# Weighing the values on quarter tiles in two PSUM banks, later in the slot, and without the loop over layers

## The reference

```python
def local_attention(q, k, v):              # 16 heads of 64, window w = 32
    ...                                    # bq: windows of 32 queries
    bk2, bv2 = (look(bk), look(bv))        # a window and the one before it: 64 keys
    sim = jnp.einsum('bhwie,bhwje->bhwij', bq, bk2) * QK_SCALE
    sim = jnp.where(mask, -jnp.finfo(sim.dtype).max, sim)
    attn = jax.nn.softmax(sim, -1)
    out = jnp.einsum('bhwij,bhwje->bhwie', attn, bv2)
    return out.reshape(b, h, n, d)
...
for i in range(DEPTH):                     # 6
    x = attn_layer(shift_tokens(x), Wqkv[i], q_scale[i], k_scale[i], Wo[i]) + x
    x = ffn_layer(shift_tokens(x), ln_g[i], ln_b[i], W1[i], b1[i], W2[i], b2[i]) + x
```

## Time and profile before

| what | value |
|---|---|
| median of 3 runs | 2080.57 us (2078.74 to 2081.38) |
| the profiled execution | 2075.03 us |
| its span, first to last instruction | 2073.2 us |
| PE busy | 1919.3 us (93%) |
| DVE busy | 1605.8 us (77%) |
| ACT busy | 1390.0 us (67%) |
| POOL busy | 1341.2 us (65%) |

### The profile page before, as it was taken

The page is one execution under the profiler, slowest core; times in us unless marked ns, Lnnn a source line. Parts: engine busy times, 40 slices in busy tenths (PEclk is TensorE's granted clock), DMA queues, the critical chain, the costliest instruction groups (busy, mean ns, idle before and its releaser), DMA issues. The chain is left out here.

```text
span 2073.2 us, 70057 instructions
## 1 busy us (share of the span) xinstructions
PE 1919.3 (93%) x26905; PEld 1408.2 (68%) x26905; DVE 1605.8 (77%) x3109; ACT 1390.0 (67%) x2780; POOL 1341.2 (65%) x1402
## 2 busy tenths in 40 slices
PE   4999997899999999989989999998999899999995
PEld 3667665777767767767767677676777676777762
DVE  5666665788898878888868988688888788888773
ACT  2665663677757767776767577676777675777762
POOL 0000004998788767878767977688878678787840
PEclk9999999999999999999999999999999999999996
DMA  2000000443424334333343243343333433333330
GB/s 95 2 1 0 0 30 6 115 107 101 123 76 105 96 92 119 90 90 96 98 112 100 75 104 98 90 121 88 91 100 96 116 93 79 103 99 96 98 91 20
DMA packets 190633, 171.70 MB, mean 83 GB/s; under 512 B 32160, under 2 KB 186440, under 8 KB 190152
## 3 DMA queue, kind: packets, MB, share of 16 engines
q1 hardware_dynamic: 190280, 167.02, 30.7%
HBM read 21.14 MB, written 1.05 MB: 11 GB/s over the span
## 5 line engine op out<-in xcount | busy, mean ns | idle before, releaser
L407 POOL TENSOR_TENSOR z_raw<-rot_u,rot_v 128x256 f32<-128x256 f32 x768 | 552.2, 743 | 186.3 <-DVE rot_v L1016 183.8
L422 POOL TENSOR_TENSOR z_norm<-probs_t,z_raw 128x512 f32<-128x512 f32 x384 | 493.1, 1306 | 110.4 <-DVE probs_t L1065 110.4
L1015 DVE TENSOR_TENSOR rot_u<-bank,tabs 128x512 f32<-128x512 f32 x384 | 263.1, 685 | 183.3 <-ACT sq L521 180.2
L781 PE MATMUL bank<-x_high,w_high 128*128 128x256 f32 x768 | 304.4, 396 | 2.8 <-issue 1.1
L553 ACT ACTIVATE pair_bank<-pair_bank 128x512 f32<-128x512 f32 x192 | 111.8, 582 | 256.1 <-DVE pair_bank L998 255.9
L521 ACT ACTIVATE sq<-bank 128x512 f32<-128x512 f32 x384 | 225.6, 589 | 53.9 <-PE bank L783 44.4
L1016 DVE TENSOR_TENSOR rot_v<-bank,tabs 128x512 f32<-128x512 f32 x384 | 261.5, 681 | 0.0
L428 POOL TENSOR_TENSOR sqs<-sq 128x512 f32<-128x512 f32 x192 | 245.3, 1278 | 23.6 <-POOL z_norm L422 23.5
L540 ACT ACTIVATE probs_t<-bank 64x512 f32<-64x512 f32 x384 | 227.3, 592 | 45.4 <-PE bank L760 43.1
L772 PEld LDWEIGHTS bank<-probs_t,v_late 128*64 128x64 f32 x3072 | 155.5, 138 | 145.8 <-issue 145.8
L825 PE MATMUL bank<-sqs,consts 128*128 128x512 f32 x384 | 204.4, 614 | 44.5 <-POOL sqs L428 41.5
(11 more groups left out here) (153 smaller groups left out, 4545.4 us busy)
## 6 DMA issues: line engine op xcount, KB each, us to landing
zqk<-z_norm SPq DMA_DIRECT2D x1536, 64.0 KB, 2.1
v_late<-v_sb SPq DMA_DIRECT2D x192, 192.0 KB, 2.6
w_qkv<-in_L_ffn_Wqkv SPq DMA_DIRECT2D x18, 512.0 KB, 5.1
v_late<-v_sb SPq DMA_DIRECT2D x192, 32.0 KB, 2.2
wo<-in_L_ffn_Wo SPq DMA_DIRECT2D x24, 128.0 KB, 2.1
w<-in_L_ffn_W SPq DMA_DIRECT2D x12, 170.5 KB, 3.0
consts<-in_constants SPq DMA_DIRECT2D x1, 1088.0 KB, 5.1
w_qkv<-in_L_attn_w_kv_up SPq DMA_DIRECT2D x2, 512.0 KB, 6.3
```

The costliest lines, as they stand in the source:

```text
L407: a = pool.tensor_tensor(z_raw[:, parity, idx, half, :], rot_u[:, idx, half, :], rot_v[:, idx, 1 - half, :], ALU.add)
L422: a = pool.tensor_tensor(z_norm[:, parity, idx, :, :], rinv[:, idx, :].unsqueeze(1).broadcast_to([P, 2, T]), z_raw[:, parity, idx, :, :], ...
L781: pe.matmul(dst, w_high[:, j, cols], x_high[:, odd, :], start=True, stop=False)
L1015: dve.tensor_tensor(rot_u[:, idx, :, :], src, tabs[:, 2 * idx, :, :], ALU.mult)
```

## The change

Two edits are made. First, the probabilities are copied as they are, not spread among zeros, by one copy of 128 partitions; V is then weighed by 32 products in place of 16, each of 64 keys by 64 features with 32 moving columns, on four tiles of 64 by 64. The products of the lower keys' half go to `B_T`, those of the upper half to `B_K`, so ACT copies the outputs in two pieces of 256 columns. Because `B_K` is used, the products must wait until the keys in it were squared, and `weigh_windows` moves behind the MLP and the queries; on ACT the squares of the keys move ahead of the logarithm. Second, `stream` runs all slots as straight code; register arithmetic becomes constants, the `sem_inc` of `room_met` and `split_begun` and the memset of `spread` go.

```diff
-        def stream(eng, slot):
-            for k in range(FIRST, LOOP):
-                slot(k, 0)
-            with eng.Fori(0, TURNS) as r:
-                for k in range(LOOP, LOOP + LAYER):
-                    slot(k, r)
-            for k in range(LOOP, LAST - TURNS * LAYER):
-                slot(k, TURNS)
...
+        def stream(slot):
+
+            for s in range(FIRST, LAST):
+                slot(s)
...
                     act.wait_ge(S["turned"], s)
                     after(act, "lpv_done", s - 1)
-                    tiles = B_T.rearrange("p (h s c) -> p h s c", h=HG, s=TILES)
-                    for x in range(2):
-                        rows = slice(KEYS * x, KEYS * x + KEYS)
-                        a = act.activation(spread[rows, :, :, WIN * x:WIN * x + WIN], tiles[rows, :, :, :], ACT.Copy)
-                    a.then_inc(S["spread_ready"], 1)
...
+                    a = act.activation(turned_t[:, :, :], B_T.rearrange("p (h c) -> p h c", h=HG), ACT.Copy)
+                    a.then_inc(S["turned_ready"], 1)
...
+                if one:
+                    squares(s + 4, "k_prod", B_K, 1, "k_square")
                 if two:
                     m = s + 3
                     act.wait_ge(S["n_done"], m + 1)
...
-                if one:
-                    squares(s + 4, "k_prod", B_K, 1, "k_square")
...
-                    act.activation(yt[:, 2 * og:2 * og + 2, :], B_T.rearrange("p (c t) -> p c t", c=2), ACT.Copy).then_inc(S["lyt_ready"], 1)
+                    for x, bankx in enumerate((B_K, B_T)):
+                        dst = yt[:, 2 * og:2 * og + 2, :].rearrange("p c (t x n) -> p c t x n", t=TT, x=2)
+                        a = act.activation(dst[:, :, :, 1 - x, :], bankx[:, 0:T].rearrange("p (c t n) -> p c t n", c=2, t=TT), ACT.Copy)
+                    a.then_inc(S["lyt_ready"], 1)
...
-                pe.wait_ge(S["spread_ready"], n + 1)
-                for pair, tile, a in itertools.product(range(2), range(TILES), range(2)):
-                    h, t = 2 * pair + a, tile // 2
+                pe.wait_ge(S["turned_ready"], n + 1)
+                for pair, tile, a, x in itertools.product(range(2), range(TILES), range(2), range(2)):
+                    h, t, rows = 2 * pair + a, tile // 2, slice(KEYS * x, KEYS * x + KEYS)
                     f = slice(g * GW + h * D, g * GW + (h + 1) * D)
-                    y = B_T[D * a:D * a + D, T * pair:T * pair + T].rearrange("p (t x s c) -> p t s x c", t=TT, x=2, s=2)
-                    mm = pe.matmul(y[:, t, tile % 2, :, :], (v_sb if tile % 2 else v_late)[:, odd, t, f], spread[:, h, tile, :], start=True, stop=True,
-                                   tile_position=(0, D * a), skip_group_check=True)
+                    at = P * pair + WIN * tile
+                    mm = pe.matmul((B_T, B_K)[x][D * a:D * a + D, at:at + WIN], (v_sb if tile % 2 else v_late)[rows, odd, t, f],
+                                   turned_t[rows, h, WIN * tile:WIN * tile + WIN], start=True, stop=True, tile_position=(KEYS * x, D * a), skip_group_check=True)
...
-                if four:
-                    weigh_windows(s - 1, unit_of(k - 1, r), (k - 1) % G, (k - 1) // G % 2)
...
                 if one:
                     project(s + 4, 0, B_Q, g, odd, "lq_done", ("q_prod", "q_square"))
+                if four:
+                    if one:
+                        pe.wait_ge(S["k_square"], s + 5)
+                    weigh_windows(s - 1, (s - 1) // G, (s - 1) % G, (s - 1) // G % 2)
                 if one:
                     values(s + 4, g, odd)
```

More of the change, by code:

```diff
@@ L367, in slot @@
-                if k == LAYER + 14:
-                    sp.wait_ge(S["mlp_done"], (NB // 2) * (r + 1))
-                    sp.sem_inc(S["room_met"], 1)
-                    down_weights(r + 1)
-            stream(sp, slot)
+                    out_weights(0, s + 1)
+                l = layer_begun(s, LAYER - 14)
+                if l:
+                    sp.wait_ge(S["split_done"], G * l)
+                    qkv_weights(l)
+                for g in range(G):
+                    l = layer_begun(s, LAYER - 1 + g)
+                    if l:
+                        sp.wait_ge(S["lwo_done"], s - 1)
+                        out_weights(l, g)
@@ L374, in _ @@
+            stream(slot)
             sp.wait_ge(S["scores_done"], GROUPS)
@@ L428, in slot @@
                     pool.tensor_tensor(sqs[:, :, :], sq[:, :, 0, :], sq[:, :, 1, :], ALU.add).then_inc(S["sums_ready"], 1)
-                    rotated(s + 4, k % 2, 0, "q_prod", "q_summed")
-                if not isinstance(r, int) and LAYER - 7 <= k < LAYER - 7 + G:
-                    g = k + 7 - LAYER
-                    if g == 0:
-                        pool.wait_ge(S["w_in"], 16 * 3 * (r + 2))
-                    pool.wait_ge(S["lv_done"], s + 4)
-                    pool.sem_inc(S["split_begun"], 1)
-                    split_weights(r + 1, g)
-            pool.wait_ge(S["pv_done"], STEPS)
-            pool.memset(spread[:, :, :, :], 0.0).then_inc(S["spread_zero"], 1)
+                    rotated(s + 4, s % 2, 0, "q_prod", "q_summed")
+                for g in range(G):
+                    l = layer_begun(s, LAYER - 7 + g)
+                    if l:
+                        pool.wait_ge(S["w_in"], 16 * 3 * (l + 1))
+                        pool.wait_ge(S["lv_done"], s + 4)
+                        split_weights(l, g)
             pool.wait_ge(S["w_in"], 16 * 3)
@@ L442, in _ @@
                 split_weights(0, g)
-            stream(pool, slot)
+            stream(slot)
         @block.scalar
@@ L604, in _ @@
             gate_biases(0)
-            act.wait_ge(S["spread_zero"], 2)
-            stream(act, slot)
+            act.wait_ge(S["late_zero"], 1)
+            stream(slot)
         @block.tensor
@@ L899, in _ @@
                 pt_taken(STEPS - 1, h)
-            stream(pe, slot)
+            stream(slot)
             for p in range(PAIRS):
@@ L1036, in out_biases, with slot @@
                 dve.wait_ge(S["out_bias_ready"], l + 1)
-            def slot(k, r):
-                s, g = LAYER * r + k, k % G
-                one, two, three = active(k, r, -4, GROUPS - 4), active(k, r, -3, GROUPS - 3), active(k, r, 0, GROUPS)
-                if k % (2 * G) == 5 and mlp_active(k, r, 21):
-                    p, b = mlp_of(k - 21, r), 2 * ((k - 21) // (2 * G)) % NB
+            def slot(s):
+                g = s % G
+                one, two, three = active(s, -4, GROUPS - 4), active(s, -3, GROUPS - 3), active(s, 0, GROUPS)
+                if mlp_slot(s, 21):
+                    p = (s - 21) // (2 * G)
+                    b = 2 * p % NB
                     dve.wait_ge(S["mlp_done"], p + 1)
@@ L1101, in _ @@
             turn(causal, 0, ("post",))
-            stream(dve, slot)
+            stream(slot)
             dve.wait_ge(S["mlp_res"], MLPS)
```

250 lines of the change are left out of this document (120 added, 130 removed).

## The result

The changed kernel takes 2107.16 us, median of 4 runs (2104.17 to 2116.16), beside 2079.65 for the kernel before in the same session (2073.41 to 2081.38). The ratio is 1.0145, 95% interval 1.0108 to 1.0182: 1.45% slower. The profiled execution took 2106.53 us, with a span of 2104.7 against 2073.2.

A forecast was written before the change was run, and what follows sets the result against it. PE, busy 93%, was taken to bound the kernel, each slot being its work plus small waits. Loop -31, new waits +70, first slots and tables +10 gave +49: 2124 beside the profiled 2075.03, median 2130 us, range 2055 to 2170.

The forecast's parts named there:

- Loop: Where the stream jumps back: straight code saves 7.8 us at each of four jumps, -31 us; bounds 0 and -31.
- Block: The weighing's 64 pairs on four tiles: each turn bound by its 64-column load, 1.06 us, so halved matmuls buy nothing.
- The weakest step: Weighing block: the load-bound turn, resting on a slope of mean durations; named weakest together with slots 0 to 3.
- The short block: Rival, 0.14: four tiles give the scores' rate, block 0.78 us in place of 1.06, 24 us less in all, 2106.
- the long one: Rival, 0.05: loads or tiles of the two row halves take turns, block 1.9 us; 2290 at most, 2210 likelier.
- My second rival: The weighing block near its lower bound, the scores' 64 pairs in 0.78 us, by the skill's promised speedup; chance 0.14.
- Slot by slot, per eight: New PE waits after the weighing moves behind MLP and queries: +3.2 us per eight slots, +70 over 22 eights.
- The waits: PE waits for gate copy (slots 6, 7, about 0.8), keys' squares (slot 5, 0.7), output copy (starts of slots 5, 6).
- 0.8 is new: Slot 6, before the centre product: 1.54 us from the weighing's end, values hide 0.72, leaving 0.8 of new wait.
- First slots and tables: First slots, and five times where DVE writes new rotary tables and the logarithm waits for late keys: +10 us.
- The rival "faster": Chance 0.18: new waits replace 1.9 us of old ones per eight; 2089, 2064 or 2050 us; eights below 68.0 mean faster.

The follow-up runs named there:

- the two halvings: Changed kernel with loads of 32 columns in place of 64: 2084.14 us; changed kernel with 16 moving columns in place of 32: 2109.13 us; one run each.

## Why the prediction was right, and by how much it missed

The forecast was 2130 us, +2.4%; measured were 2107.16, +1.45%. The direction and both mechanisms hold; the sum over the slots was too large.

**Loop: -31.** Measured were -29.6 in the jumps' slots, and -31.5 between the medians of straight code and the kernel before. Right.

**Block: 1.06 us, bound by its loads.** Measured 1.065, and the two halvings show the reason. The weakest step was the surest. The short block and the long one fall. The Trainium skill, "TensorEngine Tiling (Array Packing)", section "Theoretical Speedup", gives up to double where a dimension is 64 or less. Counted by pairs the trace agrees: 1.082 / 32 = 33.8 ns a pair before, 16.6 after. But there are twice as many pairs, since a product no longer serves two windows at once, and so the block gained 1.6% (1.082 to 1.065 us). My second rival had read a rate of pairs as a time of the block.

**Slot by slot, per eight.** The first column is the prediction's, the second is the typical slot after less before:

| slots | forecast | measured |
|---|---|---|
| 4 | +0.23 | +0.08 |
| 5 | +0.95 | +0.80 |
| 6 | +0.67 | +0.60 |
| 7 | +0.82 | +0.75 |
| 0 and 1 | +0.3 | +0.16 |
| 2 and 3 | +0.2 | +0.13 |
| sum | +3.2 | +2.5 |

Every term has the right sign and is too large, by 0.07 to 0.15. One mis-sized step stands in slots 4, 6 and 7: I took 1.08 us out of PE's chain ahead of MLP and queries. A tiled block costs something at its edges as well. The norm's next product comes after 0.86 us when it is the MLP (1545.40 to 1546.26), and came after 0.95 when it was the block; the queries begin 0.46 after the MLP's product (1546.26 to 1546.72), before it was 0.56 (1103.69 to 1104.25):

```profile
1104.25 0.68 PE L781 MATMUL bank<-x_high,w_high 128*128 128x256 f32 x1
```

That is 1.27 us, not 1.08; back in come 0.08, as the block begins 0.20 after the last product of the queries (1556.58 to 1556.78) instead of 0.12, and 0.10 in the values behind it (1541.23 to 1541.45, where 0.12 is usual). PE's work stays the same in sum, but 1.27 - 0.08 = 1.19 left the front of the slot, so the block starts 0.1 earlier than I worked out, and with it all that waits for its end. In slot 7 I had queries done at 5.79; the block starts at 1565.58 - 1559.87 = 5.71. In slot 4 it starts at 1540.16 - 1532.73 = 7.43 where I had 7.63, of which the edges are half. In slot 6 two errors nearly cancel: I had queries done at 6.24, but the kernel before starts its values 7.50 into that slot (1106.09 to 1113.59), so that it should have been 7.50 - 1.08 = 6.42; the block starts at 1556.78 - 1550.59 = 6.19, as the wait for POOL's sums fell there from 0.36 to 0.22 besides. Slot 5 hangs on the squares of the keys and not on PE's chain (below), and slots 0 to 3 I have not followed row by row. The Trainium skill, "TensorEngine Tiling (Array Packing)", section "Key Properties", says that changing the tiling mode drains TensorE. It gives no price; the rows here put 0.08 to 0.1 us on an edge, and whether the drain is the cause they can't show.

**The waits.** The waits for the gate copy and for the squares of the keys are there; the one for the output copy doesn't show as I had said. The chain from the block's end to the centre product was forecast at 1.54 and is 1559.36 - 1557.85 = 1.51. I said "0.8 is new"; the profile prints 0.54, since it counts from the modelled end of the last product, but the distance between the products grew by 0.70, as the kernel with the gate copy first shows. The wait for the squares of the keys in slot 5 was forecast at 0.7 and is 0.60: ACT starts them 5.77 after the slot's start (forecast 5.8), and they release PE 0.65 later (forecast 0.58 and a wake of 0.16):

```profile
1547.94 0.60 ACT L505 ACTIVATE sq<-bank 128x512 f32<-128x512 f32 x1 [0.60 <-DVE rot_v L1000]
```

So the block began 6.42 into slot 5 and not 6.54, most of that slot's 0.15. The waits for the output copy I had put at the starts of slots 5 and 6; the view prints none there. From the block's end to the next transposes it is 1542.17 - 1541.23 = 0.94 us, beside 0.96 to 0.98 in the forecast, but 0.82 of it are now values, so the wait is about 0.1 where I had 0.26.

**First slots and tables: +10.** Slots 0 to 15 grew by 3.5, and 4.6 came ahead of slot 0. The layers' last slots grew by 9.1; five times slots 2 to 7 at the typical growth make 5 x 2.36 = 11.8, so in sum the tables' transitions added nothing of their own. I had counted about 5 for them. The wait for late keys that I had named is there, 3.66 us, and the slot with it grew by 8.5 us in five; but the slot behind it shrank by 5.0, and the old wait of 1.77 went. The 4.6 isn't explained: this stretch differed by -0.4 to +5.7 us between the experiments, and straight code alone had 1.6 of it.

**The rival "faster".** It had a small true part that my sum left out. Of the 1.9 us of old waits per eight, the 0.27 for `yt` at the start of slot 2 went, but 0.22 for POOL's sums came in the same slot; in slot 6 the wait for the sums fell by 0.14; the 0.87 of slot 1 stayed. In sum the wait for the sums did not fall, 41.5 us before and 44.8 after. The 8.8 us in front of the values were not given back either: the wait for the squares took their place. And an eight is 69.10 us, above the 68.0 at which that rival decides. Its reason was wrong where I had said so: the gate wait hangs on the block's own end, and no earliness of another engine moves it; only another order does.

In sum the miss is 2130 - 2107 = 23 us. Per eight 2.5 instead of 3.2 makes 22 x 0.7 = 15 of it, and 5.5 is the step from the profiled execution to the median, which I had added; the changed kernel's profiled run, 2106.53, lies at its median. The last 2 or 3 are the first slots and tables, less the loop.

## What to carry to other kernels

When a product is moved on PE, look on every other in-order engine for what stands behind its consumer: here a copy whose input had long been ready stood behind the copy of the moved block, and that cost 32 to 34 us, which swapping the two gave back. Before splitting products onto more tiles, ask whether stream or load sets the turn: here twice the pairs on twice the tiles, with the load's columns as they were, took the same time, and the borrowed bank brought a wait with it. Cost a loop's jump by the distance of the repeated parts, not by the first idle stretch in it: that was 14.0 of the 29.6 us.

## What the runs showed of the hardware

- 64 pairs of f32 load and matmul on four tiles of 64 by 64 take 1.065 us, 16.6 ns a pair; with loads of 32 columns 0.686 us, 10.7 ns a pair; with half the moving columns 1.052. The Trainium skill, "TensorE: Matmul & The Clock Gate", section "Wait — 56ns, not 53.3ns?", gives a floor of about 25 ns from start to start. On tiles side by side it doesn't show.
- The tiled block's edges cost PE 0.08 to 0.1 us each. In the kernel before, the step from the norm took 0.95 instead of 0.86, and that from the MLP's product behind the block 0.56 instead of 0.46; in the changed kernel the two edges took 0.20 instead of 0.12 and 0.22 instead of 0.12.
- A jump back of this loop on all engines costs 7.4 us: 3.2 to 3.7 us of idle time, 0.5 to 1.5 us more within the scores, and a granted clock of 0.50 for the products behind it. In the changed kernel's 192 slots of straight code PE is idle for "issue" only twice ahead of the scores, 1.2 us in all, and once for 1.1 us where the stream begins, as in the kernel before.
- The long wait at the new tables has the slower clock behind it too: PE waited until 1184.77 us, and from 1186 to 1189 the granted clock was 0.50. In the kernel before it waited until 1168.82, and the clock was 0.50 from 1170 to 1176.
